# Four layers of gated attention with feed-forwards: each projected tile normalised and routed in the projection's stage, router tables loaded once, weight waits moved to the folding

## The reference, cut to what matters

```python
x = x + tanh(g_xattn[l]) * attention_l(layernorm(x), ctx)
x = x + tanh(g_ffn[l])   * feed_forward_l(layernorm(x))
```

## Time and profile before

| what | value |
|---|---|
| median of 3 runs | 2712.72 us (2711.11 to 2716.27) |
| profiled execution, its own time | 2715.86 us |
| its span, first to last instruction | 2714.0 us |
| PE busy | 2402.6 us, 89% of the span |
| DVE, ACT, POOL busy | 59%, 36%, 30% |
| mean granted PE clock | 0.883 of 2.4 GHz |
| DMA | 267.39 MB, mean 99 GB/s |

### The profile page before, as it was taken

How to read it: one execution, slowest core, us unless ns; L and a number is a source line. 1 busy time by engine, 2 the same in 40 slices (tenths; PEclk the granted TensorE clock), 3 DMA queues, 4 the chain that set the end, 5 groups by cost and what they waited for, 6 DMA issues and landing times. The chain is left out here.

```text
span 2714.0 us, 33651 instructions
## 1 busy us (share of the span) xinstructions
PE 2402.6 (89%) x11268; PEld 1714.5 (63%) x11268; DVE 1588.1 (59%) x2546; ACT 974.1 (36%) x1433; POOL 812.8 (30%) x485
## 2 busy tenths in 40 slices
PE   7777679978999999599999999748889999994998
PEld 4677579864666665465566665548646666664997
DVE  4545344427777774477778777311277777734444
ACT  3222134423444443121344444201234444422443
POOL 0222023301444443045244444110014444420332
PEclk9555789967999999699899999969679999996999
DMA  1333133526434430312343442087154434301442
GB/s 35 105 95 121 59 108 114 153 80 173 101 86 104 103 78 16 110 52 95 88 109 84 100 103 60 13 290 241 54 156 100 105 88 100 86 8 47 118 120 84
DMA packets 109660, 267.39 MB, mean 99 GB/s; under 512 B 25907, under 2 KB 62813, under 8 KB 106434
## 3 DMA queue, kind: packets, MB, share of 16 engines
q1 hardware_dynamic: 108866, 264.00, 35.4%
q0 software_dynamic: 672, 1.84, 0.2%
HBM read 219.21 MB, written 46.41 MB: 98 GB/s over the span
## 5 line engine op out<-in xcount | busy, mean ns | idle before, releaser
L1110 DVE TENSOR_REDUCE keep_top<-banks 128x1 f32<-128x500 f32 x1008 | 656.0, 675 | 270.4 <-PE banks L1049 267.6
L1168 ACT ACTIVATE att_ex<-banks 125x896 f32<-125x896 f32 x576 | 526.1, 918 | 260.4 <-PE banks L1038 238.1
L1218 POOL TENSOR_TENSOR att_acc<-att_acc,att_two 125x896 f32<-125x896 f32 x186 | 393.2, 2114 | 448.1 <-DVE att_two L1125 434.2
L1066 PE MATMUL banks<-att_ex,att_v 125*64 125x448 f32 x2304 | 464.8, 545 | 0.0
L1049 PE MATMUL banks<-keep_kh,keep_qt 128*128 128x500 f32 x1008 | 392.7, 439 | 18.4 <-DVE keep_top L1110 7.2
L1125 DVE TENSOR_TENSOR att_two<-att_ex 125x896 f32<-125x896 f32 x288 | 315.2, 1133 | 49.7 <-ACT att_ex L1168 48.5
L1038 PE MATMUL banks<-keep_qt,keep_kh 128*125 128x448 f32 x1152 | 333.6, 371 | 2.3 <-ACT att_ex L1168 2.3
L1038 PE MATMUL banks<-att_qm,att_kl 65*125 65x448 f32 x1152 | 331.8, 369 | 0.0
L1066 PEld LDWEIGHTS banks<-att_ex,att_v 125*64 125x64 f32 x2304 | 152.5, 136 | 247.8 <-issue 200.7
L1447 PE MATMUL banks<-moe_xs,moe_w 128*128 128x448 f32 x1272 | 279.7, 370 | 23.9 <-DVE moe_xs L1562 22.9
L1049 PEld LDWEIGHTS banks<-keep_kh,keep_qt 128*128 128x128 f32 x1008 | 188.4, 198 | 175.2 <-issue 85.7
(11 more groups left out here) (227 smaller groups left out, 2435.0 us busy)
## 6 DMA issues: line engine op xcount, KB each, us to landing
keep_kh<-kvt_hi SPq DMA_DIRECT2D x96, 375.0 KB, 5.0
q_rows<-mats_q SPq DMA_DIRECT2D x24, 896.0 KB, 4.0
keep_qt<-q_rows SPq DMA_DIRECT2D x48, 448.0 KB, 6.4
moe_raw<-L_experts_dram SPq DMA_DIRECT2D x53, 384.0 KB, 4.1
att_kl<-kvt_lo SPq DMA_DIRECT2D x48, 375.0 KB, 8.1
att_v<-kvn SPq DMA_DIRECT2D x24, 720.0 KB
sort_wu<-L_experts_dram SPq DMA_DIRECT2D x14, 1024.0 KB, 7.1
moe_cb<-comb_rows SPq DMA_DIRECT2D x62, 224.0 KB
```

The costliest lines, as they stand in the source:

```text
L1066: last = pe.matmul(PS[WEIGHED][64 * e:64 * e + 64, 0:HALF], v[:, s // 2, u, s % 2, :], ex[:, u % RING, e, :], start=u == 0, stop=u == UNIT ...
L1110: dve.tensor_reduce(top[:, s % 2, n // NS, n % NS:n % NS + 1], PS[6 + (PIECES * s + n) % 2][:, 0:SB], AX.X, ALU.max).then_inc(mx_done, 1)
L1168: act.activation(ex[:, u % RING], scored, ACT.Exp).then_inc(exp_done, 1)
L1218: pool.tensor_tensor(a, two[:, 0] if n == 1 else a, two[:, n % 3], ALU.add).then_inc(gathered, 1)
```

## The change

- `project_out` now does the normalising too, tile by tile: after tile t is added to x, DVE takes its statistics, ACT the square root, DVE scales it; PE turns it two tiles later, between the products, ACT copies it, and, for layers 0, 2 and 3, PE multiplies it by the router's weights into bank 7 four tiles later. The stage "normf" and the logits of `route` and `sorted_experts` are gone.
- The router's weights, the tie table, the bias and the sorting tables stay in SBUF for the whole program and are loaded in the first `normalise`.
- W is counted on one semaphore of the whole program. PE waits for it at the head of the folding; no SP list waits for it. Its larger tensors are loaded in halves (nine DMAs instead of six), and in `experts` one piece is issued behind the loads of each of the chunks 1 to 9.
- In `sorted_experts` the third tile's expert weights are issued behind the first four loads of sorted rows.
- xn is one tile for the whole program; some other buffers now share memory (`cm`, `step`, `oT`, `xh`, `h`).

```diff
+        self.arrived = G["weights_in"]
+
+        cut = ("wc", "wq", "wo") if l else ()
+        self.pieces = [(n, a, z) for n, shape in shapes.items() for a, z in (
+            ((0, shape[1] // 2), (shape[1] // 2, shape[1])) if n in cut else ((0, shape[1]),))]
+        G["weights_expected"] = self.expected = G.get("weights_expected", 0) + 16 * len(self.pieces)
...
-    def load(self, sp, loaded):
-        for n, tile in self.tiles.items():
-            sp.dma_start(tile[:], self.sources[n]).then_inc(loaded, 16)
-
-    def wait(self, sp, loaded):
-        sp.wait_ge(loaded, 16 * len(self.tiles))
-
-
-def normalise(nc, G, name, W=None, rows=None):
+    def load_piece(self, sp, i):
+        n, a, z = self.pieces[i]
+        sp.dma_start(self.tiles[n][:, a:z, :], self.sources[n][:, a:z, :]).then_inc(self.arrived, 16)
+
+    def load(self, sp):
+        for i in range(len(self.pieces)):
+            self.load_piece(sp, i)
+
+    def wait(self, pe):
+        pe.wait_ge(self.arrived, self.expected)
+
+
+def normalise(nc, G, name, W=None):
 
     x, xT, PS, ident = G["x"], G["xT"], G["PS"], G["ident"]
     with Stage(nc, name) as st:
         stats, mv = st.sb("stats", [128, NT, 6]), st.sb("mv", [128, NT, 2])
         ve, sd, r, t = (st.sb(n, [128, NT]) for n in ("ve", "sd", "r", "t"))
-        xn = st.sb("xn", [128, NT, H]) if rows is None else rows
+        xn = G["xn"]
...
                 if W:
-                    W.load(sp, weights_in)
-                    W.wait(sp, weights_in)
+                    W.load(sp)
+                    for dst, src in G["tables"]:
+                        sp.dma_start(dst, src).then_inc(G["tables_in"], 16)
...
             def _(pe):
+                W.wait(pe)
...
+    PS, x, xT, xn, ident = G["PS"], G["x"], G["xT"], G["xn"], G["ident"]
+    routed = l != 1
+    wr = G[f"wr{l}"] if routed else None
+    E = wr.shape[2] if routed else 0
...
+                def turn(t):
+                    pe.wait_ge(xn_ready, t + 1)
+                    for k in range(KC):
+                        last = pe.transpose(PS[t][:, 128 * k:128 * k + 128], xn[:, t, 128 * k:128 * k + 128], ident[:, :])
+                    last.then_inc(tr_done, 1)
+
+                def logits(t):
+                    if not routed:
+                        return
+                    if t == 0:
+                        pe.wait_ge(G["tables_in"], 16 * len(G["tables"]))
+                    pe.wait_ge(copied, t + 1)
+                    for k in range(KC):
+                        pe.matmul(PS[7][:, t * E:t * E + E], xT[:, k, 128 * t:128 * t + 128], wr[:, k, :],
+                                  start=k == 0, stop=k == KC - 1)
+
                 for t in range(NT):
                     for h in range(NP):
                         last = pe.matmul(PS[t][:, 0:H], ctxT[:, h, 128 * t:128 * t + 128], Bm[:, h, :],
                                          start=h == 0, stop=h == NP - 1)
                     last.then_inc(o_ready, 1)
+                    if t >= 2:
+                        turn(t - 2)
+                    if t >= 4:
+                        logits(t - 4)
+                turn(NT - 2)
+                for t in range(NT - 4, NT - 2):
+                    logits(t)
+                turn(NT - 1)
+                for t in range(NT - 2, NT):
+                    logits(t)
 
             @block.vector
             def _(dve):
+                c = Count(dve, chain)
                 for t in range(NT):
+                    one = slice(t, t + 1)
                     dve.wait_ge(o_ready, t + 1)
                     dve.scalar_tensor_tensor(x[:, t, :], PS[t][:, 0:H], G["tanh"][:, l:l + 1], x[:, t, :],
                                              ALU.mult, ALU.add).then_inc(x_done, 1)
+                    dve.wait_ge(x_done, t + 1)
+                    c.link(dve.bn_stats(stats[:, t, :], x[:, t, :]))
+                    c.link(dve.bn_aggr(mv[:, t, :], stats[:, t, :]))
+                    dve.tensor_scalar(ve[:, one], mv[:, t, 1:2], EPS, None, ALU.add).then_inc(var_ready, 1)
+                    dve.wait_ge(sqrt_done, t + 1)
+                    c.link(dve.reciprocal(r[:, one], sd[:, one]))
+
+                    c.link(dve.tensor_tensor(t2[:, one], r[:, one], r[:, one], ALU.mult))
+                    c.link(dve.tensor_tensor(t2[:, one], t2[:, one], ve[:, one], ALU.mult))
+                    c.link(dve.tensor_scalar(t2[:, one], t2[:, one], -0.5, 1.5, ALU.mult, ALU.add))
+                    c.link(dve.tensor_tensor(r[:, one], r[:, one], t2[:, one], ALU.mult))
+                    dve.tensor_scalar(xn[:, t, :], x[:, t, :], mv[:, t, 0:1], r[:, one],
+                                      ALU.subtract, ALU.mult).then_inc(xn_ready, 1)
+
+            @block.scalar
+            def _(act):
+                def copy(t):
+                    act.wait_ge(tr_done, t + 1)
+                    act.activation(xT[:, :, 128 * t:128 * t + 128],
+                                   PS[t][:, 0:KC * 128].rearrange("p (k n) -> p k n", k=KC), ACT.Copy).then_inc(copied, 1)
+
+                for t in range(NT):
+                    act.wait_ge(var_ready, t + 1)
+                    act.activation(sd[:, t:t + 1], ve[:, t:t + 1], ACT.Sqrt).then_inc(sqrt_done, 1)
+                    if t >= 3:
+                        copy(t - 3)
+                for t in range(NT - 3, NT):
+                    copy(t)
...
-                for dst, src in loads:
-                    sp.dma_start(dst, src).then_inc(in_w, 16)
                 sp.wait_ge(tr_copied, 2)
                 halves = ((0, E), (E, rows)) if rows > E else ((0, E // 2), (E // 2, E))
                 for a, z in halves:
@@ -1296,12 +1366,6 @@
 
             @block.tensor
             def _(pe):
-                pe.wait_ge(in_w, 16 * len(loads))
-                for t in range(NT):
-                    for k in range(KC):
-                        last = pe.matmul(PS[0][:, t * E:t * E + E], xT[:, k, 128 * t:128 * t + 128], wr[:, k, :],
-                                         start=k == 0, stop=k == KC - 1)
-                last.then_inc(lg_ready, 1)
...
-                if W:
-                    W.load(sp, weights_in)
-                    W.wait(sp, weights_in)
+                    if W and 1 <= c <= len(W.pieces):
+                        W.load_piece(sp, c - 1)
...
-                for dst, src in ((wr[:, :, :], G["L2_router"]), (before[:, :], G["before"]), (tables[:, :], G["sorting"])):
-                    sp.dma_start(dst, src).then_inc(in_w, 16)
                 sp.wait_ge(zeroed, 1)
                 sp.dma_start(G["sorted_x"].rearrange("(n p) d -> p n d", p=128),
                              zeros.unsqueeze(1).broadcast_to([128, TILES, H])).then_inc(cleared, 16)
-                W.load(sp, weights_in)
+                W.load(sp)
...
-                for i in range(RINGW):
+                for i in range(RINGW - 1):
                     load_ups(i)
                     load_downs(i)
                 sp.wait_ge(scattered, 16 * NT)
                 for i in range(RINGX):
                     load_rows(i)
+                load_ups(RINGW - 1)
+                load_downs(RINGW - 1)
...
-                W.wait(sp, weights_in)
 
             @block.tensor
             def _(pe):
-                pe.wait_ge(in_w, 48)
-                for t in range(NT):
-                    for k in range(KC):
-                        last = pe.matmul(PS[7][:, t * E1:t * E1 + E1], xT[:, k, 128 * t:128 * t + 128], wr[:, k, :],
-                                         start=k == 0, stop=k == KC - 1)
-                last.then_inc(lg_ready, 1)
...
-                W.load(sp, weights_in)
-                W.wait(sp, weights_in)
+                W.load(sp)
...
+        G["xn"] = sb("xn", [128, NT, H])
+        for l, E in ((0, 16), (2, E1), (3, 16)):
+            G[f"wr{l}"] = sb(f"wr{l}", [128, KC, E])
+        G["tie"], G["bias"] = sb("tie", [128, 256]), sb("bias", [128, 16])
+        G["count"], G["sort"] = sb("count", [128, 128]), sb("sort", [128, E1 + NT + E1 * E1 + TILES])
+        G["tables"] = [(G[f"wr{l}"][:, :, :], G[f"L{l}_router"]) for l in (0, 2, 3)] + [
+            (G["tie"][:, :], G["tie16"]), (G["bias"][:, :], G["L3_bias"].broadcast_to([128, 16])),
+            (G["count"][:, :], G["before"]), (G["sort"][:, :], G["sorting"])]
+        G["tables_in"] = stack.enter_context(nc.semaphore("tables_in"))
...
-        with Stage(nc, "rows2") as st:
-            xn = st.sb("xn", [128, NT, H])
-            normalise(nc, G, "normf2", rows=xn)
-            sorted_experts(nc, G, W, xn)
+        sorted_experts(nc, G, W)
         return
-    normalise(nc, G, f"normf{l}")
```

56 lines of the change are left out of this document (26 added, 30 removed).

## The result

The changed kernel takes 2668.98 us (median of 4 runs, 2663.04 to 2670.43); beside it the kernel before took 2714.49 us (4 runs, 2711.11 to 2720.81). The ratio is 0.9824 with a 95% interval of 0.9805 to 0.9843. The profiled execution of the changed kernel is its fastest run: 2663.04 us, span 2661.2.

A forecast was written before the change was run, and what follows sets the result against it. PE is busy 89% of the span, so gains lie mainly in its idle 11%. Terms 12.0 + 13.3 + 4.6 + 5.2 + 2.0 + 8.3 = 45.4 us give 2670.5 (profiled) or 2667.3 (median); forecast 2669, range 2661 to 2684.

The forecast's parts named there:

- Layer 0: From the projection's first product to the logits: 44.84 us before, 32.8 forecast, a gain of 12.0 us.
- Layer 3: From the projection's first product to the logits: 46.09 us before, 32.8 forecast, a gain of 13.3 us.
- turn 6, its drain and copy, the last logits 0.45: Projection's tail after DVE's chain ends at 30.9: 0.22, about 0.7 and 0.45 us, PE ending at 32.5.
- Layer 1: Projection, without logits, to SP's first DMA of the next stage: 36.11 us before, 31.5 forecast, a gain of 4.6 us.
- Tables at no cost: Seven small DMAs in the first normalise, some 0.45 us each on SP's queue, cost 0; under 2 us otherwise.
- Weight waits: Waits for folding weights before normalising shrink to 0.3 us: gains 5.2 after layer 0's experts, 2.0 after the quantised layer.
- Just in time: Layer 0's experts: a chunk behind a weight piece lands after 8.3 us, used 8.6 after issue; cost 0, bound 5 us.
- Sorted rows: Layer 2's sort: queue starts 4.3 us sooner, third tile's weights save 3.7, tables 0.3; together 8.3 us.
- the first (small PE instructions keep their half-clock price): Turns and logits in the projections stay at half-clock price: 11 us lost, time 2680, chance 0.10.
- The second: Transfers answer less: the sort gains 2.9 instead of 8.3 us, or pieces delay chunks; 2674 to 2680, chance 0.12.
- the third (the clock falls in the projections): Turns and logits among products drop the clock to 0.50: 104 us over four stages, time 2773, chance 0.03.
- the fourth (half of the projections' gain lost): Tile 6's tail or a stage border grows and half the projections' gain goes: time 2686, chance 0.05.

The follow-up runs named there:

- the repeat: The changed kernel measured once more with nothing edited: 2671.12 us, ratio 0.9851.
- the versions beyond the change: The changed kernel with layer 2's folding weights moved from ahead of everything to behind, between or around the sort's tiles and stores: 2653.51 to 2669.71 us.

## Why the prediction was right

The forecast was 2669, the median is 2668.98; so close is luck, since single terms were off by up to 2 us and cancelled. By its steps, in profiled executions (first, and the repeat in brackets):

- **Layer 0**, 12.0 forecast: 11.1 (11.4). **Layer 3**, 13.3: 12.8 (12.6). DVE's chain of 3.0 us was 3.00, the turns 0.22 a tile as taken, the logits 0.36 a tile instead of 0.45. The stage is 33.3 to 33.8 instead of 32.8, and two steps make the difference. The flow up to the last product's end is 310.08 - 281.73 = 28.35 where 27.9 was worked out. And the step "turn 6, its drain and copy, the last logits 0.45" priced the tail at full clock, while the clock is back at 0.50: from the end of the chain to the logits' copy it took 2.4 us instead of 1.9. (The prediction's own terms, 30.9 + 0.22 + 0.7 + 0.45, make 32.3 where it writes 32.5 for PE's end, which hid 0.2 of this. DVE's extra small instructions are 36 a stage, 144 in all, not 42.)
- **Layer 1**, 4.6 forecast: 36.11 - 31.58 = 4.5.
- **Tables at no cost** in the first normalise held: the first folding starts 0.03 us earlier than before. Their share in what was won, which the prediction did not split off, is 4.7 of 11.1 us in layer 0.
- **Weight waits**, 5.2 and 2.0: 5.4 and 1.7. No chunk came so late that it cost anything: the first layer's experts have the length they had (188.8 us, 189.2 before). "Just in time", 8.3 of 8.6 us, was close: in the first profile ACT's copy of a chunk waits for a load only before the first chunk of each expert stage, in the repeat it waits once more, for 1.1 us, and in the kernel with the logits behind the projection four times more, for up to 2.2 us, with the stage at 188.8 us in both. (The 0.3 us of a plain border, for which the prediction names rows 7, comes from rows 6: 1.3 us over four borders.) What the prediction left out is that a wait gone can be worth more than its length: behind the quantised layer it also gave 1.7 us or more in the next stage, by the clock.
- **Sorted rows**, 8.3 forecast: 10.0. Of this 3.9 is the earlier zeros (4.3 taken) and 3.7 the third tile (3.7 taken, 3.69 measured by itself). The term that was too small is the 0.3 for the tables' loads: 44.76 - 42.37 = 2.4 us remain between the kernel before and the changed kernel with the third tile put back in front. Before, the scatter also came 15.8 us after the zeros and now comes after 9.1, and the rows were asked for after 31.7 instead of 24.5; how the 2.4 us divide was not tried.
- **The logits in layer 2 are worth nothing**, since the backlog bounds: held, with rows at 72.11 and 72.31 us with and without them in the stage behind.
- **Sum**, 45.4: these terms give, before rounding, 45.6 in the first profile and 45.7 in the repeat, and the sort from its first tile on is 1.0 (0.1) us shorter. The first profile is shorter by 6 us more, in unchanged stages. Of these 1.7 (3.3 in the repeat) belong to layer 2's folding and so to the change; most of the rest, like the 2.6 us before layer 0's queries, did not repeat.

Of the rivals, the first (small PE instructions keep their half-clock price) is wrong in the flow, 0.09 and 0.11 us apart, and right for the tail alone. The second did not come about (the sort gained more than forecast, no chunk was delayed), nor did the third (the clock falls in the projections) or the fourth (half of the projections' gain lost). One of the signs that the prediction named as wrong, rows that wait for the scatter rather than the queue, shows only in the versions beyond the change: with the weights out of the way the rows are asked for 22.6 us after the zeros and turned 2.2 us later.

On the price of a turn the Trainium skill, "TensorE: Matmul & The Clock Gate", section "Part 4: PE-mode transpose", has about 275 ns. The trace prints 0.27 as a turn's median too, but a pair of turns delays what stands behind it by 0.22, and the sum by the distance of starts was the one that held.

## What to carry to other kernels

Work that waits at a border can cost twice, as idle time and as the half clock of what follows; the tables' waits and the one behind the quantised layer showed it, the one behind layer 0's experts did not, so read the granted clock at the start of the next stage. Put small PE work into a dense run of products. Where transfers bound a start, count every byte that stands ahead in the queue, whoever needs it, and move what is needed last behind it, but not ahead of small stores or beside a gather on which everything waits. A part that only joins a queue that is bound elsewhere (the logits in layer 2) gains nothing there.

## What was not expected of the hardware

- The same 28 logits took 6.16, 3.88 and 5.69 us: behind turns and a rest of 3.6 us, behind 14 turns and a rest of 0.7, and behind a rest of 2.7, two turns and a rest of 0.7. Behind the quantised layer 2 us of rest less ahead of the normalisation made the folding 1.7 to 3.7 us shorter. Each goes with how long the granted clock was 1.00 from the start on.
- One 0.13 MB store behind 7.34 MB of loads of the same queue stood 18.7 us in DVE's way; a gather of another queue beside the same loads landed after 10.5 us instead of 2.7.
- With nine weight pieces between the tiles' own loads, a piece of 1 MB landed 15.3 us after its issue, and each tile from the eighth on waited some 1 to 1.9 us for its weights, though the pieces with the first four tiles had cost nothing.
